# Gathering the rows of the first four expert tiles straight to their places, and moving the remaining gathers, stores and sums of a GNN + top-2 MoE kernel

## The chip, the cores and the metric

The kernel runs on one core of one Trainium2 chip. The metric is the device time of one execution in microseconds (us); lower is better. Engines are named as in the profile: PE (TensorE), DVE (VectorE), ACT (ScalarE), POOL (GpSimd), SP (SyncE, which here only issues DMAs).

## The reference

Two layers on 3125 nodes of 256 features:

```
x = x + segment_sum(einsum('ni,roi->rno', layernorm(x), w)[type, src], dst) + bias     # 53125 edges, 8 relations
n = layernorm(x)
probs = softmax(n @ gate_w + gate_b); top-2 of 16 experts, renormalised
out_e = (silu(n @ w1[e]) * (n @ w2[e])) @ w3[e]                                         # hidden 512
x = x + sum over the two chosen experts of weight * out_e
```

## The kernel before

The first two thirds (up to about 628 us) aggregate the messages of the edges, compute the second layer's normalised rows and gate logits, write these rows to the DRAM table x2_tab and choose the experts. The change does not touch them. It touches the expert stage behind them.

**Tiles.** Each (token, expert) pair has a slot; each expert's slots are padded to whole tiles of 128 rows. Experts are handled in an order of ranks: experts 0 and 1, then the others by number, the two with most tokens last. With the drawn inputs the routing of the reference gives 58 tiles, and the number of tiles up to and including rank 0, 1, 2, ... 15 is

```
rank       0  1  2   3   4   5   6   7   8   9  10  11  12  13  14  15
tiles to   3  6  9  14  16  18  23  26  29  33  37  38  43  45  50  58
```

**A tile j on PE** (expert_tile in the tensor block): turn_hid(j-1) transposes the previous tile's gated rows (line 1536); up(j) multiplies tile j's rows with w1 and w2, 12 matmul pieces (line 1528); turn_xs(j+1) transposes the next tile's rows (line 1494); down(j-1) multiplies the previous tile's gated rows with w3 (line 1510). Before up(j) PE waits for split12 of the tile's expert, before down(j-1) for split3.

**On DVE** for tile j: low_hid(j-1) (line 1253, the low part of the turned gated rows), the product hid(j) (line 1263), low_xs(j+1) (line 1243), copy_y(j-1) from PSUM to the one buffer y_sb (line 1249), which waits until the store of y of tile j-2 has landed. **On ACT** for tile j: high_hid(j-1) (line 744), silu (line 753), high_xs(j+1) (line 739), load_xs(j+2) with its argument counted from that call, that is the load of tile j+3's rows from the DRAM table xs_tab (line 735), and store_y(j-1), which waits for copy_y(j-1) and issues its store to y_tab (line 761).

**Rows.** POOL gathers rows from x2_tab with indirect DMAs, one per tile. Tiles 0 and 1 go straight to the buffers xs (line 572). All tiles, 0 and 1 included, go in "octs" of eight to a buffer (gather_oct: an index copy on line 560, eight gathers on line 564), from which SP stores them in two halves to xs_tab (store_oct, line 476); ACT's load_xs reads them back one at a time. gather_oct(q) waits for the second store of oct q-1.

**Weights.** For each rank e from 2 on, POOL runs in this order: the octs from oct_end[e-1] to oct_end[e]-1, then split_expert(e), which cuts the raw weights into a high and a low part (lines 551 and 553; first the w1 and w2 part, signalling split12, then the w3 part, signalling split3). The first part waits for the raw weights and for the up of the last tile of rank e-2, whose buffer it takes. SP runs in this order: load_expert(e) (three DMAs, line 445) once split e-2 is done, then the stores of the same octs, each of which it waits for. Rank 0 and 1 are split by ACT and DVE at the start (split_first, line 1198).

**Behind the octs** POOL gathers, 25 times each, the y rows of every token's lower and higher slot (lines 602 and 615). DVE adds the first set to acc (add_first, line 1312; 25 in all, 6 or 7 behind each of the last four tiles), ACT copies the sums to PSUM (keep_sum, line 788), DVE adds the second set (line 1331), SP and ACT store the output (lines 501 and 797).

oct_end of a rank is (tiles to + 7) >> 3 for ranks 2 to 14 and (58 + 11) >> 3 for rank 15; for ranks 0 and 1 it is 1. So oct 0 stands ahead of everything and octs 1 to 7 stand ahead of the splits of ranks 2, 5, 7, 9, 12, 14 and 15.

Of the kernel before, what the change touches and what calls it, by code (L numbers as in the profile page):

```python
# [29 lines left out]
I32 = mybir.dt.int32  # L30
ALU = mybir.AluOpType
# [3 lines left out]
P = 128  # L35
NODES, DIM, RELS = 3125, 256, 8
EDGES = 53125
EXPERTS, HIDDEN = 16, 512
# [4 lines left out]
TILES = NODES // TP  # L43
# [31 lines left out]
SLOTS = SLOT_TILES * P  # L75
AHEAD = 3
OCT = 8
HALF_OCT = OCT // 2
OCTS = -(-(SLOT_TILES + AHEAD) // OCT)
XS_TILES = OCTS * OCT  # L80
ZT = 7
# [3 lines left out]
LAST_PAIRS = 2  # L85
# [9 lines left out]
def build(nc, x, src, dst, etype, w_rel, b_rel, gate_w, gate_b, w1, w2, w3, out):  # L95
# [5 lines left out]
    with ExitStack() as ctx:  # L101
        def sb(name, shape, dt=F32):
            return ctx.enter_context(nc.sbuf_tensor(name, shape, dt))

        def sem(name):
            return ctx.enter_context(nc.semaphore(name))
# [130 lines left out]
        slot_hot = got_room[:, got_hots:got_hots + 2 * TILES * SLOT_TILES].rearrange("p (n h) -> p n h", h=SLOT_TILES)  # L237
        token = sb("token", [P, XS_TILES], I32)
        first_idx = sb("first_idx", [P, 2], I32)
        oct_idx = sb("oct_idx", [P, OCT], I32)  # L240
# [114 lines left out]
        slot_free = sem("slot_free")  # L355
        xs_first = [sem(f"xs_first{n}") for n in range(2)]
        xs_in = [sem(f"xs_in{n}") for n in range(2)]
# [148 lines left out]
        def _(pool):  # L506
# [50 lines left out]
            def gather_oct(q):  # L557
                pool.wait_ge(xs_stored, (q * 2 + 1) * 16)
                pool.sem_inc(slot_free, 1)
                nc.gpsimd.tensor_copy(oct_idx[:, :], token[:, bass.ds(q * OCT, OCT)]).then_inc(oct_ready, 1)  # L560
                pool.wait_ge(oct_ready, q + 1)
                pool.sem_inc(slot_free, 1)
                for u in range(OCT):
                    nc.gpsimd.indirect_dma_start(  # L564
                        xg[:, u, :], None, x2_tab,
                        bass.IndirectOffsetOnAxis(ap=oct_idx[:, u:u + 1], axis=0)).then_inc(oct_got[u // HALF_OCT], 16)
# [54 lines left out]
        def _(act):  # L621

            for free in (moved_on, tail_clear, x2_kept):
                act.sem_inc(free, 1)
            act.sem_inc(y_stored, 16)
            act.wait_ge(zero_set, 1)

# [105 lines left out]
            def load_xs(j, s):  # L733
                act.wait_ge(xs_stored, (j // HALF_OCT + 2) * 16)
                act.dma_start(xs[:, s, :], xs_tab[bass.ds(j * P, P), :]).then_inc(xs_in[s], 16)

            def high_xs(j, s):
                act.wait_ge(xs_turned, j + 1)
                nc.scalar.copy(xsT[:, 0, :, :], ps[:, XS_BANK, 0:DIM].rearrange("p (k n) -> p k n", k=KT)).then_inc(xsT_high, 1)
                load_xs(j + 2, s)  # L740
# [5 lines left out]
            def expert_tile(i, u, first=False):  # L746
# [18 lines left out]
            final_j = act.value_load(final[0:1, 0:1], min_val=0, max_val=SLOT_TILES - 1)  # L765
            pairs = act.value_load(pairs_i[0:1, 0:1], min_val=EXPERTS // 2, max_val=SLOT_TILES // 2)
            high_xs(0, 0)
            act.wait_ge(pos_done, 1)
            expert_tile(0, 0, first=True)
            expert_tile(0, 1)  # L770
            with act.Fori(1, pairs) as i:
                for u in range(2):
                    expert_tile(i, u)
            act.wait_ge(y_done, final_j + 1)
            high_hid(final_j)
            store_y(final_j)
            act.wait_ge(xs_in[0], (pairs + 1) * 16)
            act.wait_ge(xs_in[1], pairs * 16)
# [24 lines left out]
        def _(dve):  # L803
            steps = [0]

            def step(ins):

                steps[0] += 1
                ins.then_inc(vec_step, 1)
                dve.wait_ge(vec_step, steps[0])  # L810
# [371 lines left out]
            dve.wait_ge(inv_summed, 1)  # L1182
            v.tensor_scalar(first_idx[:, :], ps[:, INV_BANK, 0:2], float(MID_TOKEN), None, ALU.add).then_inc(token_done, 1)
            v.tensor_scalar(token[:, 0:SLOT_TILES], ps[:, INV_BANK, 0:SLOT_TILES], float(MID_TOKEN), None, ALU.add).then_inc(token_done, 1)
# [129 lines left out]

            early = dve.value_load(early_i[0:1, 0:1], min_val=EXPERTS // 2 - LAST_PAIRS, max_val=SLOT_TILES // 2 - LAST_PAIRS)
            with dve.Fori(3, early) as i:
# [19 lines left out]
        def _(pe):  # L1336
# [150 lines left out]

            def turn_xs(i, u, first=False):
                if first:
                    pe.wait_ge(xs_first[u], 16)  # L1490
                else:
                    pe.wait_ge(xs_in[u], i * 16)
                for k in range(KT):
                    last = nc.tensor.transpose(ps[:, XS_BANK, k * P:(k + 1) * P], xs[:, u, k * P:(k + 1) * P], ident[:, :])
                last.then_inc(xs_turned, 1)
# [42 lines left out]

            def expert_tile(i, u, first=False):
# [11 lines left out]
                turn_xs(i + u, 1 - u, first=first)  # L1551
# [10 lines left out]
            expert_tile(0, 1)  # L1562
            with pe.Fori(1, pairs) as i:
                for u in range(2):
                    expert_tile(i, u)
# [22 lines left out]
```

## Time and profile before

| what | value |
|---|---|
| three runs | 974.35, 977.85, 988.51 us; median 977.85 us |
| profiled execution | 975.37 us, of which the span from the first to the last instruction is 973.7 us |
| share of the span busy | PE 78%, POOL 68%, DVE 52%, ACT 27% |
| mean granted TensorE clock | 0.887 of full speed |

The span is what the profile's times are counted in; 1.7 us of the execution's time lie around it. A timeline row gives start, duration (us), engine, line, operation, output<-input, and in brackets how long the engine had been idle and what ended that.

### The profile page before, as it was taken

The page shows a single profiled execution, that of the slowest core. Times are in us where ns is not written, and L with a number is a line of the kernel's source. Part 1 is how long each engine was busy: PE and PEld are TensorE (multiplying, and loading weights), DVE is VectorE, ACT ScalarE, POOL GpSimd, SP SyncE. Part 2 cuts the span into 40 slices and gives each one's busy share as a digit, 9 for nine tenths or more (in the row PEclk, how much of TensorE's full clock was granted, in tenths as well). Part 3 has the DMA queues.
Part 4 walks back from the last instruction along what each step waited for, and adds up shares of the span by engine and source line. Part 5 has one row for each costly group of instructions (what it writes and reads, how often), then busy time and mean ns, then how long its engine had stood idle before and what let it go on. Part 6 is the DMA issues. An engine that isn't in the chain of part 4 may idle for free.

```text
span 973.7 us, 18213 instructions
## 1 busy us (share of the span) xinstructions
PE 755.4 (78%) x4527; PEld 633.7 (65%) x4528; DVE 504.2 (52%) x1473; ACT 263.0 (27%) x397; POOL 663.7 (68%) x621
## 2 busy tenths in 40 slices
PE   0446787977779888778888878268999999999981
PEld 0434576766658676666667657257888888888861
DVE  6776444545464444546444576866444344444474
ACT  4821222223222222222222222312322232322223
POOL 1077777777777777777777770156768678688775
PEclk9765998989889798988889999569999999999995
DMA  8534444444454333343334332148465665656457
GB/s 206 177 100 144 141 145 141 141 144 140 141 175 130 103 107 102 105 131 103 107 102 132 104 103 99 64 149 277 132 207 169 204 202 181 209 174 221 140 149 221
DMA packets 93343, 144.16 MB, mean 148 GB/s; under 512 B 13335, under 2 KB 67563, under 8 KB 93322
## 3 DMA queue, kind: packets, MB, share of 16 engines
q0 software_dynamic: 25968, 70.94, 25.1%
q1 hardware_dynamic: 49856, 57.31, 18.4%
q10 hardware_dynamic: 17498, 15.68, 5.0%
q8 instruction: 7, 0.11, 0.1%
q14 instruction: 14, 0.11, 0.0%
HBM read 109.90 MB, written 33.98 MB: 148 GB/s over the span
## 4 chain that ended last, share of the span: by engine, by line
PE 48%; DMA 14%; issue 12%; POOL 9%; DVE 8%; DVEq 3%; ACT 3%; ACTq 1%; SPq 0%; POOLq 0%
PE ps L1390 16%; PE ps L1528 12%; PE ps L1378 9%; PE ps L1510 7%; DMA got<-x_tab,idx 7%; POOL got L528 5%; DMA y_tab<-ffn 4%; PE ps L1536 2%; POOL part L553 2%; DMA acc<-in_x 2%; ACT store L683 1%; PE ps L1420 1%; DVE hot L947 1%; POOL x_sb L564 1%; DVE store L965 1%
## 5 line engine op out<-in xcount | busy, mean ns | idle before, releaser
L528 POOL DMA_INDIRECT got<-x_tab,idx x425 | 405.1, 953 | 172.3 <-issue 153.7
L1378 PE MATMUL ps<-hot,got 125*128 125x256 f16 x1700 | 235.1, 301 | 112.4 <-DMA got<-x_tab,idx 90.7
L1378 PEld LDWEIGHTS ps<-hot,got 125*128 125x128 f16 x1700 | 176.3, 106 | 166.9 <-issue 113.3
L965 DVE TENSOR_TENSOR store<-store,ps 128x512 f32 x150 | 102.6, 684 | 237.0 <-PE ps L1378 209.4
L1390 PE MATMUL ps<-part,store 128*128 128x256 f32 x800 | 190.5, 398 | 0.5 <-DVE acc L978 0.5
L1528 PE MATMUL ps<-part,operands 128*128 x696 | 181.2, 410 | 3.2 <-POOL part L553 2.0
L1390 PEld LDWEIGHTS ps<-part,store 128*128 128x128 f32 x800 | 159.4, 202 | 22.9 <-issue 0.5
L1528 PEld LDWEIGHTS ps<-part,operands 128*128 128x128 f32 x696 | 130.2, 193 | 31.3 <-issue 4.0
L947 DVE TENSOR_SCALAR hot<-key_row,pass,drel 125x256 f16<-125x256 f16 x425 | 123.1, 357 | 10.1 <-issue 10.1
L1510 PE MATMUL ps<-part,operands 128*128 x696 | 100.4, 294 | 13.7 <-DVE operands L1253 13.1
L666 ACT ACTIVATE dev<-mv,eps 125x1 f32<-125x1 f32 x25 | 7.4, 295 | 356.1 <-DVE mv L985 356.1
L1510 PEld LDWEIGHTS ps<-part,operands 128*128 128x128 f32 x696 | 89.2, 193 | 16.5 <-issue 16.5
L553 POOL TENSOR_TENSOR part<-store,part 128x2048 fp32r<-128x2048 f32 (+1 forms) x28 | 98.2, 3507 | 2.3
L564 POOL DMA_INDIRECT x_sb<-x_tab,oct_idx x64 | 61.8, 965 | 23.4 <-issue 16.5
L1253 DVE TENSOR_TENSOR operands<-ps,operands 128x512 fp32r<-128x512 f32 x58 | 40.1, 691 | 71.5 <-ACT operands L744 71.4
L744 ACT CAST operands<-ps 128x512 fp32r<-128x512 f32 x58 | 34.1, 587 | 158.2 <-DVE ffn L1249 140.6
L683 ACT COPY store<-store (+1 forms) x24 | 54.2, 2259 | 50.9 <-DVE store L965 50.9
L551 POOL TENSOR_SCALAR part<-store 128x2048 fp32r<-128x2048 f32 (+1 forms) x28 | 42.0, 1500 | 36.5 <-PE ps L1528 16.5
L1263 DVE TENSOR_TENSOR ffn<-ffn,ps 128x512 f32<-128x512 f32 x58 | 39.8, 685 | 38.8 <-PE ps L1528 32.5
L1249 DVE COPY ffn<-ps 128x256 f32<-128x256 f32 x58 | 24.6, 425 | 57.6 <-PE ps L1510 42.3
L661 ACT COPY store<-zero 128x2000 f32 (+1 forms) x25 | 46.8, 1874 | 0.0
L1536 PE MATMUL ps<-ident,ffn 128*128 128x128 f32 x232 | 35.7, 277 | 7.2 <-DVE ffn L1263 7.2
(225 smaller groups left out, 580.7 us busy)
## 6 DMA issues: line engine op xcount, KB each, us to landing
store<-in_L_ffn_w SPq DMA_DIRECT2D x48, 512.0 KB, 5.1
xs_tab<-x_sb SPq DMA_DIRECT2D x16, 512.0 KB, 3.3
y_tab<-ffn SPq DMA_DIRECT2D x9, 896.0 KB
ffn<-xs_tab ACTq DMA_DIRECT2D x59, 128.0 KB
y_tab<-ffn ACTq DMA_DIRECT2D x58, 128.0 KB
got<-x_tab,idx POOLq DMA_INDIRECT x425, 2.8
acc<-in_x SPq DMA_DIRECT2D x5, 560.0 KB
x_tab<-got SPq DMA_DIRECT2D x5, 560.0 KB
```

The lines of the kernel that those rows point to most:

```text
L528: nc.gpsimd.indirect_dma_start(got[:, c, :], None, x_tab, bass.IndirectOffsetOnAxis(ap=idx[:, c:c + 1], axis=0)).then_inc(gathered[c], 16)
L553: nc.gpsimd.tensor_tensor(part[:, 2 * k + 1, at:at + cols], whole, high.bitcast(F32), ALU.subtract).then_inc(done, 1)
L564: nc.gpsimd.indirect_dma_start(xg[:, u, :], None, x2_tab, bass.IndirectOffsetOnAxis(ap=oct_idx[:, u:u + 1], axis=0)).then_inc(oct_got[u // ...
L661: nc.scalar.copy(buffer(i, SPAN - TP, SPAN), zero[:, 0:1].unsqueeze(1).to_broadcast([P, KT * RELS, TP])).then_inc(tail_clear, 1)
L683: nc.scalar.copy(buffer(i + 1, 0, SPAN - TP), buffer(i, TP, SPAN)).then_inc(moved_on, 1)
L947: v.tensor_scalar(hot[0:CE, g % HOT, c - GROUPS[g][0], :], key_row[0:CE, :], pass0[0:CE, 0:1], drel[0:CE, bass.ds(turn * TC + c, 1)], ALU. ...
L965: v.tensor_tensor(window, window, ps[:, WIN_BANK[g], :].rearrange("p (q n) -> p q n", n=WIN), ALU.add).then_inc(win_added, 1)
L1378: last = mm(ps[:, WIN_BANK[g], k * KEYS:(k + 1) * KEYS], got[0:CE, c, a * DIM + k * P:a * DIM + (k + 1) * P], hot[0:CE, g % HOT, c - c0, : ...
L1390: last = mm(ps[:, bank, 0:DIM], sums[:, at, k, r, 0:P], wT[:, k, r * DIM:(r + 1) * DIM], start=(r == 0 and k == 0), stop=(r == RELS - 1 an ...
L1510: last = mm(ps[:, Y_BANK, 0:DIM], hidT[:, a, k, :], part3[:, bass.ds(at + b, 1), k, :].rearrange("p a n -> p (a n)"), start=(k == 0 and a ...
L1528: last = mm(ps[:, UP_BANK + w, :], xsT[:, a, k, :], part12[:, bass.ds(at + b, 1), w, k, :].rearrange("p a n -> p (a n)"), start=(k == 0 an ...
L1536: last = nc.tensor.transpose(ps[:, HID_BANK, k * P:(k + 1) * P], hid[:, k * P:(k + 1) * P], ident[:, :])
```

## The change

Five edits in the expert stage. (1) Four tiles instead of two are gathered straight to buffers (two new ones, xs_ahead), and oct q holds tiles 4+8q to 11+8q. PE takes tiles 0 to 3 from the buffers; ACT's first load is that of tile 4, issued in tile 1, and in tile 0 ACT loads nothing. (2) oct_end becomes max(tiles to + 4, 8) >> 3 for ranks 0 to 14 and (58 + 4) >> 3 = 7 for rank 15: seven octs, 1 to 6 standing ahead of the splits of ranks 3, 6, 8, 10, 13 and 15. (3) ACT's store_y(j-2) stands behind high_hid(j-1) in tile j, no longer at the end of tile j-1. (4) The loads past the last tile are left out. (5) DVE's 25 add_first stand behind the last low_hid: three ahead of the last copy_y, 22 behind it.

```diff
-AHEAD = 3
+DIRECT = 4
-OCTS = -(-(SLOT_TILES + AHEAD) // OCT)
+OCTS = -(-(SLOT_TILES + 2 - DIRECT) // OCT)
...
-                nc.gpsimd.tensor_copy(oct_idx[:, :], token[:, bass.ds(q * OCT, OCT)]).then_inc(oct_ready, 1)
+                nc.gpsimd.tensor_copy(oct_idx[:, :], token[:, bass.ds(q * OCT + DIRECT, OCT)]).then_inc(oct_ready, 1)
...
-            for u in range(2):
+            for u in range(DIRECT):
                 nc.gpsimd.indirect_dma_start(
-                    xs[:, u, :], None, x2_tab,
+                    xs[:, u, :] if u < 2 else xs_ahead[:, u - 2, :], None, x2_tab,
                     bass.IndirectOffsetOnAxis(ap=first_idx[:, u:u + 1], axis=0)).then_inc(xs_first[u], 16)
...
             def load_xs(j, s):
-                act.wait_ge(xs_stored, (j // HALF_OCT + 2) * 16)
+                act.wait_ge(xs_stored, (j // HALF_OCT + 1) * 16)
...
-                high_xs(j + 1, 1 - u)
-                if not first:
-                    store_y(j - 1)
+                if not first and not second:
+                    store_y(j - 2)
                 act.wait_ge(up1_done, j + 1)
                 act.wait_ge(hid_ready, j)
                 nc.scalar.activation(gate, ps[:, UP_BANK, :], ACT.Silu).then_inc(gate_ready, 1)
                 act.wait_ge(up2_done, j + 1)
+                high_xs(j + 1, 1 - u, load=load and not first)
...
             act.wait_ge(y_done, final_j + 1)
             high_hid(final_j)
+            store_y(final_j - 1)
             store_y(final_j)
...
-                v.tensor_scalar(oct_f[:, EXPERTS - 1:], t_rank[:, EXPERTS - 1:EXPERTS], float(OCT + AHEAD), None, ALU.add)
-                step(v.tensor_scalar(oct_f[:, 0:EXPERTS - 1], t_rank[:, 0:EXPERTS - 1], float(OCT - 1), None, ALU.add))
+                v.tensor_scalar(oct_f[:, EXPERTS - 1:], half_f[:, :], 2.0, float(OCT - DIRECT), ALU.mult, ALU.add)
+                step(v.tensor_scalar(oct_f[:, 0:EXPERTS - 1], t_rank[:, 0:EXPERTS - 1], float(OCT - DIRECT), float(OCT), ALU.add, ALU.max))
...
-            last_tiles = 2 * LAST_PAIRS
-            for n in range(last_tiles):
-                expert_tile(early + n // 2, n % 2)
-                for t in range(TILES * n // last_tiles, TILES * (n + 1) // last_tiles):
-                    add_first(t)
             low_hid(final_j)
+            for t in range(3):
+                add_first(t)
             copy_y(final_j)
+            for t in range(3, TILES):
+                add_first(t)
...
-            turn_xs(0, 0, first=True)
-            expert_tile(0, 0, first=True)
-            expert_tile(0, 1)
-            with pe.Fori(1, pairs) as i:
+            turn_xs(0, 0, direct=True)
+            expert_tile(0, 0, first=True, direct=True)
+            expert_tile(0, 1, direct=True)
+            expert_tile(1, 0, direct=True)
+            expert_tile(1, 1)
+            with pe.Fori(2, pairs) as i:
```

## Rows read from the trace of the kernel before

**Rows 1.** The page's first part: busy us, share of the span, count of instructions.
```profile
PE 755.4 (78%) x4527; PEld 633.7 (65%) x4528; DVE 504.2 (52%) x1473; ACT 263.0 (27%) x397; POOL 663.7 (68%) x621
```

**Rows 2.** Timeline, PE: up of tiles 1, 9, 13, 18 and 57.
```profile
646.91 5.26 PE L1528 MATMUL ps<-part,operands 128*128 x12
...
693.75 3.05 PE L1528 MATMUL ps<-part,operands 128*128 x12
...
713.41 3.05 PE L1528 MATMUL ps<-part,operands 128*128 x12
...
740.11 3.07 PE L1528 MATMUL ps<-part,operands 128*128 x12
...
939.90 3.05 PE L1528 MATMUL ps<-part,operands 128*128 x12
```

**Rows 3.** Timeline, POOL: index copies of octs 2 and 3, and their splits.
```profile
702.34 0.19 POOL L560 COPY oct_idx<-token 128x8 int32 x1
...
716.74 1.92 POOL L551 TENSOR_SCALAR part<-store 128x2048 fp32r<-128x2048 f32 x1 [3.62 <-issue]
718.75 4.62 POOL L553 TENSOR_TENSOR part<-store,part 128x2048 fp32r<-128x2048 f32 x1
...
730.34 1.91 POOL L551 TENSOR_SCALAR part<-store 128x2048 fp32r<-128x2048 f32 x1 [3.46 <-DMA store<-in_L_ffn_w]
...
740.36 0.18 POOL L560 COPY oct_idx<-token 128x8 int32 x1
...
751.15 1.92 POOL L551 TENSOR_SCALAR part<-store 128x2048 fp32r<-128x2048 f32 x1
...
758.87 2.39 POOL L553 TENSOR_TENSOR part<-store,part 128x1024 fp32r<-128x1024 f32 x1
```

**Rows 4.** Timeline, start of the stage: POOL's copy, SP's load, split of rank 2.
```profile
649.37 0.43 POOL L560 COPY oct_idx<-token 128x8 int32 x1 [5.15 <-DMA xs_tab<-x_sb]
...
651.83 2.36 SPq L445 DMA_DIRECT2D store<-in_L_ffn_w  x3
...
662.32 1.94 POOL L551 TENSOR_SCALAR part<-store 128x2048 fp32r<-128x2048 f32 x1 [2.00 <-DMA store<-in_L_ffn_w]
```

**Rows 5.** Timeline of SP alone: loads of ranks 6 and 7.
```profile
723.07 6.07 SPq L445 DMA_DIRECT2D store<-in_L_ffn_w  x6
```

**Rows 6.** Timeline, start of the stage: two gathers of POOL beside DVE's subtractions.
```profile
629.72 2.27 DVE L1198 TENSOR_TENSOR part<-store,part 128x2048 fp32r<-128x2048 f32 x1
...
630.34 2.48 POOL L572 DMA_INDIRECT ffn<-x_tab,first_idx  x1 [0.30 <-issue]
...
638.02 1.30 DVE L1198 TENSOR_TENSOR part<-store,part 128x1024 fp32r<-128x1024 f32 x1
638.06 0.94 POOL L564 DMA_INDIRECT x_sb<-x_tab,oct_idx  x1 [0.30 <-issue]
```

**Rows 7.** Timeline, start of the stage: DVE's tables and ACT's first silu.
```profile
640.92 0.06 DVE L1238 MEMSET oct_end<- 1x2 int32 x1
...
644.77 0.60 ACT L753 ACTIVATE ffn<-ps 128x512 f32<-128x512 f32 x1 [11.88 <-DMA xs_tab<-x_sb]
```

**Rows 8.** Waits, 640 to 954 us: us in total, times, longest.
```profile
DVE ffn L1249 <- DMA y_tab<-ffn: 15.3, 8, 3.0
```

**Rows 9.** Timeline, end: POOL's first and last y gather, last tile, final adds.
```profile
903.96 1.00 POOL L602 DMA_INDIRECT x_sb<-y_tab,pos  x1 [0.15 <-issue]
...
945.73 2.85 DVE L1312 SCALAR_TENSOR_TENSOR acc<-x_sb,wts,acc 125x256 f32<-125x256 f32 x7
...
949.50 2.93 PE L1510 MATMUL ps<-part,operands 128*128 x12 [3.81 <-DVE operands L1253]
...
954.19 7.37 DVE L1331 SCALAR_TENSOR_TENSOR acc<-store,wts,ps 125x256 f32<-125x256 f32 x17 [1.20 <-ACT ps L788]
...
966.10 0.95 POOL L615 DMA_INDIRECT store<-y_tab,pos  x1 [0.30 <-issue]
...
970.83 0.48 DVE L1331 SCALAR_TENSOR_TENSOR acc<-store,wts,ps 125x256 f32<-125x256 f32 x1 [1.15 <-DMA store<-y_tab,pos]
```

More of the change, by code:

```diff
@@ L237, in build @@
         slot_hot = got_room[:, got_hots:got_hots + 2 * TILES * SLOT_TILES].rearrange("p (n h) -> p n h", h=SLOT_TILES)
-        token = sb("token", [P, XS_TILES], I32)
-        first_idx = sb("first_idx", [P, 2], I32)
+        token = sb("token", [P, XS_TILES + DIRECT], I32)
+        first_idx = sb("first_idx", [P, DIRECT], I32)
+        xs_ahead = sb("xs_ahead", [P, DIRECT - 2, DIM])
         oct_idx = sb("oct_idx", [P, OCT], I32)
@@ L355, in build @@
         slot_free = sem("slot_free")
-        xs_first = [sem(f"xs_first{n}") for n in range(2)]
+        xs_first = [sem(f"xs_first{n}") for n in range(DIRECT)]
         xs_in = [sem(f"xs_in{n}") for n in range(2)]
@@ L625, in _ @@
             act.sem_inc(y_stored, 16)
+            for n in range(2):
+                act.sem_inc(xs_in[n], (n + 1) * 16)
             act.wait_ge(zero_set, 1)
@@ L733, in load_xs, with high_xs @@
             def load_xs(j, s):
-                act.wait_ge(xs_stored, (j // HALF_OCT + 2) * 16)
-                act.dma_start(xs[:, s, :], xs_tab[bass.ds(j * P, P), :]).then_inc(xs_in[s], 16)
-            def high_xs(j, s):
+                act.wait_ge(xs_stored, (j // HALF_OCT + 1) * 16)
+                at = nc.s_assert_within(j - DIRECT, 0, XS_TILES - 1, skip_runtime_bounds_check_because="pairs are counted from 1")
+                act.dma_start(xs[:, s, :], xs_tab[bass.ds(at * P, P), :]).then_inc(xs_in[s], 16)
+            def high_xs(j, s, load=True):
                 act.wait_ge(xs_turned, j + 1)
                 nc.scalar.copy(xsT[:, 0, :, :], ps[:, XS_BANK, 0:DIM].rearrange("p (k n) -> p k n", k=KT)).then_inc(xsT_high, 1)
-                load_xs(j + 2, s)
+                if load:
+                    load_xs(j + 2, s)
             def high_hid(j):
@@ L744, in high_hid, with expert_tile @@
                 nc.scalar.copy(hidT[:, 0, :, :], ps[:, HID_BANK, :].rearrange("p (k n) -> p k n", k=HT)).then_inc(hidT_high, 1)
-            def expert_tile(i, u, first=False):
+            def expert_tile(i, u, first=False, second=False, load=True):
                 j = i * 2 + u
@@ L764, in _ @@
             act.sem_inc(tiles_begun, 1)
-            final_j = act.value_load(final[0:1, 0:1], min_val=0, max_val=SLOT_TILES - 1)
+            final_j = act.value_load(final[0:1, 0:1], min_val=EXPERTS - 1, max_val=SLOT_TILES - 1)
             pairs = act.value_load(pairs_i[0:1, 0:1], min_val=EXPERTS // 2, max_val=SLOT_TILES // 2)
-            high_xs(0, 0)
+            early = act.value_load(early_i[0:1, 0:1], min_val=EXPERTS // 2 - LAST_PAIRS, max_val=SLOT_TILES // 2 - LAST_PAIRS)
+            high_xs(0, 0, load=False)
             act.wait_ge(pos_done, 1)
             expert_tile(0, 0, first=True)
-            expert_tile(0, 1)
-            with act.Fori(1, pairs) as i:
+            expert_tile(0, 1, second=True)
+            with act.Fori(1, early + (LAST_PAIRS - 1)) as i:
                 for u in range(2):
                     expert_tile(i, u)
+            for u in range(2):
+                expert_tile(early + (LAST_PAIRS - 1), u, load=False)
             act.wait_ge(y_done, final_j + 1)
             high_hid(final_j)
+            store_y(final_j - 1)
             store_y(final_j)
-            act.wait_ge(xs_in[0], (pairs + 1) * 16)
+            act.wait_ge(xs_in[0], pairs * 16)
             act.wait_ge(xs_in[1], pairs * 16)
@@ L1182, in _ @@
             dve.wait_ge(inv_summed, 1)
-            v.tensor_scalar(first_idx[:, :], ps[:, INV_BANK, 0:2], float(MID_TOKEN), None, ALU.add).then_inc(token_done, 1)
+            v.tensor_scalar(first_idx[:, :], ps[:, INV_BANK, 0:DIRECT], float(MID_TOKEN), None, ALU.add).then_inc(token_done, 1)
             v.tensor_scalar(token[:, 0:SLOT_TILES], ps[:, INV_BANK, 0:SLOT_TILES], float(MID_TOKEN), None, ALU.add).then_inc(token_done, 1)
@@ L1313, in add_first @@
                                        in1=acc[:, t, :], op0=ALU.mult, op1=ALU.add).then_inc(part_done, 1)
-            early = dve.value_load(early_i[0:1, 0:1], min_val=EXPERTS // 2 - LAST_PAIRS, max_val=SLOT_TILES // 2 - LAST_PAIRS)
-            with dve.Fori(3, early) as i:
+            with dve.Fori(3, pairs) as i:
                 for u in range(2):
                     expert_tile(i, u)
-            last_tiles = 2 * LAST_PAIRS
-            for n in range(last_tiles):
-                expert_tile(early + n // 2, n % 2)
-                for t in range(TILES * n // last_tiles, TILES * (n + 1) // last_tiles):
-                    add_first(t)
             low_hid(final_j)
+            for t in range(3):
+                add_first(t)
             copy_y(final_j)
+            for t in range(3, TILES):
+                add_first(t)
             for t in range(TILES):
@@ L1485, in _, with turn_xs @@
             pe.wait_ge(owner_done, 3)
-            def turn_xs(i, u, first=False):
-                if first:
-                    pe.wait_ge(xs_first[u], 16)
-                else:
-                    pe.wait_ge(xs_in[u], i * 16)
+            def turn_xs(i, u, direct=False):
+                if direct:
+                    pe.wait_ge(xs_first[2 * i + u], 16)
+                else:
+                    pe.wait_ge(xs_in[u], (i + u) * 16)
+                rows = xs_ahead if direct and i else xs
                 for k in range(KT):
-                    last = nc.tensor.transpose(ps[:, XS_BANK, k * P:(k + 1) * P], xs[:, u, k * P:(k + 1) * P], ident[:, :])
+                    last = nc.tensor.transpose(ps[:, XS_BANK, k * P:(k + 1) * P], rows[:, u, k * P:(k + 1) * P], ident[:, :])
                 last.then_inc(xs_turned, 1)
@@ L1537, in turn_hid, with expert_tile @@
                 last.then_inc(hid_turned, 1)
-            def expert_tile(i, u, first=False):
+            def expert_tile(i, u, first=False, direct=False):
                 j = i * 2 + u
@@ L1550, in expert_tile @@
                 owner_at(coming, j + 1)
-                turn_xs(i + u, 1 - u, first=first)
+                turn_xs(i + u, 1 - u, direct=direct)
                 if not first:
@@ L1559, in _ @@
             owner_at(this, 0)
-            turn_xs(0, 0, first=True)
-            expert_tile(0, 0, first=True)
-            expert_tile(0, 1)
-            with pe.Fori(1, pairs) as i:
+            turn_xs(0, 0, direct=True)
[4 more added lines that the diff above has]
+            with pe.Fori(2, pairs) as i:
                 for u in range(2):
```

## The prediction

> **What bounds the kernel now.** I read the page first: PE is busy for 78% of the span and POOL for 68% [rows 1], so in the expert stage either may set the end. The timeline of PE then gives the pace. Between tile 18 (740.11) and tile 57 (939.90) 199.8 us pass for 39 tiles [rows 2]; where nothing stalls, tile 9 to tile 13 takes 19.66 us, 4.9 us a tile, so 191.2 of the 199.8 us are PE's own pace and 8.6 us are stalls. Stretches between waits are PE-bound; the stalls come from two sides. One is the store of y: DVE's copy waited 8 times, 15.3 us in all, for a store that had not landed [rows 8]. The other is POOL.
>
> POOL's timeline shows its prices. An oct takes 10.8 us from its index copy (740.36) to the next split (751.15). A split takes 10.1 us (751.15 to 758.87 + 2.39), and its first part, which releases PE's up, 6.6 us (716.74 to 718.75 + 4.62) [rows 3]. From an oct's index copy (702.34) through its two stores and SP's next load (723.07) to the split that needs this load (730.34) it is 28.0 us [rows 3, 5]; it is one of four such passages (octs 2 to 5), between 26.1 and 28.0 us, and I use 27. At the end POOL issues 50 gathers without a gap from 903.96 to 966.10, and the last adds and output stores follow [rows 9]. So PE stops at 952.4 but the kernel ends at 973.7: **the end is set by when POOL is through its last split**, 0.2 us before 903.96, as long as PE is not much later.
>
> **The start (edits 1 and 3).** ACT's first silu waited 11.88 us for oct 0's first store, because the load of tile 2 stood ahead of it in ACT's queue. That load is gone. DVE's product of tile 0 then waits only for DVE itself, which is busy with tables to 640.98, instead of for the silu that ends at 645.37 [rows 7]: 4.4 us earlier. From tile 1 (646.91) to tile 9 (693.75) 46.8 us pass for 8 tiles [rows 2]; 39.2 are pace, so 7.6 were lost there, 2.2 of them to the clock (below) and the rest to y stores that met rank 2's load and to DVE's weight sums. With the store behind high_hid and the first y stores ahead of that load, I take 3.6 of these back: 8 us of lead in all, between 4.4 and 10. Alone this would be the gain.
>
> **The octs (edits 1 and 2).** The two extra gathers stand ahead of oct 0: 2 x 1.27 us (49 steps from 903.96 to 966.10 [rows 9]). The eight gathers of oct 0 now lie beside DVE's two subtractions of split_first(1). One gather beside such an operation took 2.48 us and another 0.94 us [rows 6], so this costs 0 to 1.5 us for each of two; I take 1.5 in all. Oct 0 is stored 4 us later, and SP, which waits for it, issues rank 2's load at 655.8 instead of 651.83 [rows 4].
>
> The Trainium skill's page "SBUF — State Buffer", section "SBUF: two separate sides", says GpSimd cannot write a gather's descriptors while a VectorE operation holds the shared port pair. The 2.48 us gather that ends 0.8 us after the subtraction agrees, the 0.94 us one beside the subtraction of 638.02 does not. By the rule both subtractions would block, and the load would be issued 1.5 us later than I take.
>
> Now the order matters. Before, oct 1 was gathered while rank 2's load was still under way and cost nothing: copy at 649.37, split 2 at 662.32 [rows 4]. After the change rank 2 has 9 + 4 = 13, 13 >> 3 = 1, so oct 1 stands behind split 2 and ahead of split 3, and POOL stands idle for the load. The load took 10.5 us to its split beside oct 1's gathers and 7.3 us elsewhere (723.07 to 730.34) [rows 3 to 5]; I take 7.5 us, split 2 at 663.3. Then 10.2 (split 2) + 10.8 (oct 1) + 6.6 (first part of split 3) + 0.2 puts **up of tile 9 at 691.1**. PE would want it at 685.7 (8 us ahead of 693.75): a new wait of 5.4 us that takes most of the lead, 2.6 us left against 693.75 [rows 2]. After such an idle time PE ran at 1.2 GHz: the up of tile 1, behind a long wait, took 5.26 us against 3.05 us at 2.4 GHz, and the last down took 2.93 us after 3.81 us idle [rows 2, 9]. That is 2.2 us more. Tile 13 is at 691.1 + 2.2 + 19.6 = 712.9, where it was before (713.41).
>
> Split 5 needs the up of tile 13 (tiles to rank 3 are 14), so it starts 3.3 us later, 716.2, as before. Before, oct 2 lay ahead of it in idle time. Now it lies behind it, ahead of split 6: 716.2 + 10.2 + 10.8 + 6.6 + 0.3 puts **up of tile 18 at 744.1, 4.0 us later than before**, after 6.7 us of idle PE, and again 2.2 us at 1.2 GHz: 6.2 us behind.
>
> From there the cycle runs oct, store, load, split (27.0), the even split (10.2), next oct: oct 2 at 726.4, oct 3 at 763.6, oct 4 at 800.8, split 11 at 827.8, split 12 at 838.0, oct 5 at 848.2, split 14 at 875.2 with its first part done at 881.8. Splits 7 to 13 are ready when PE comes, within 1 us. Tile 45 needs split 14: 882.1, against PE's own 744.1 + 2.2 + 27 x 4.9 = 878.6. Then tile 57 at 940.9 (before 939.90). Split 14 ends at 885.4, oct 6 and split 15 take 10.8 + 10.2: **POOL is free at 906.4, 2.6 us later** than before, although it has one oct (10.8 us) less to do: it has exchanged that for idle time behind loads.
>
> **The store behind high_hid (edit 3).** After a late copy ACT issued the store and then high_hid, and DVE's low part waited for that; now DVE goes on at once, but each store is issued later by high_hid's time, and so lands later. Its worth lies between a small loss and the 8.6 us of stalls. I count the y stalls behind tile 18 as gone, since I added none to the sum; this is not seen at the end, because the splits bind there.
>
> **The end (edit 5).** The last four tiles lose their adds: at least most of the 3.81 us that PE stood idle ahead of the last down, behind seven adds [rows 9]. Before, the last down began 9.6 us after tile 57's up; without that wait, and at 2.4 GHz, it ends near 950 instead of 952.4. One copy later, 22 adds of 0.41 us (2.85 us for seven) take 9.0 us, to 959.6, and 25 final adds of 0.43 us (7.37 us for 17) take 10.8, to 970.4. The last gather is issued at 966.10 + 2.6 = 968.7, and its add starts 4.7 us later as before (970.83), at 973.4. So POOL is still last, by 3 us, and the output stores, which started at 954 and now start at 960, are packed closer: 0.8 us, taken between 0 and 2.
>
> **Sum.** 2.6 + 0.8 = 3.4 us on the profiled execution's 975.37: 978.8 us. The three runs' median, 977.85, is 2.5 above the profiled execution, but with one run at 988.51 in it; I put half of that on: 980.
>
> **The rivals.** (A) *The lead is kept, faster.* Rank 2's load is issued 1.5 us earlier and PE's clock does not fall at tiles 9 and 18: 1.5 + 4.4 us off the chain, POOL free some 3 to 5 us before 903.96. If the new waits are shorter too, the freed oct shows, POOL would be done near 895, PE's last copy near 945, and the 22 adds in front of 25 final ones become the bound: 945 + 9.0 + 10.8, 2.9 for the last output store (970.83 to 973.7) and 1.7 around the span, that is 969.4; 971 with the packed stores. For it: POOL loses an oct and 8 us at the start are real. Against it: both octs 1 and 2 leave idle time for busy time [rows 3, 4].
>
> (B) *The loads are slow, slower.* Everything behind hangs on rank 2's load and on four store-load passages. If the first takes the 10.5 us it took before [rows 4] and each passage the 28.0 us of the row instead of 27, that is 3 + 4 us, and with the port rule 1.5 more: 988. It decides once POOL is free after 908. To pass 2% (997) POOL would have to be free after 922; no row carries that.
>
> (C) *Nothing reaches the end.* POOL is free within 1 us of 903.8 since losses and the oct cancel, or the moved adds are the only thing seen: 976 to 978.
>
> **Chances.** Forecast 0.45, A 0.2, B 0.15, C 0.2. The range 969 to 990 holds the forecast, C, most of A and B. A change of 2% is about what a measurement of this kernel can tell from none; 958 and 997 are beyond all cases but their mixtures: faster 0.04, same 0.92, slower 0.04.
>
> **What would show it.** First silu near 638 and tile 1's up near 642.5: the start. A PE wait of 4 to 7 us ahead of tile 9 ended by POOL's subtraction of split 3, another ahead of tile 18, with an up of 5 us behind each: the octs' places. First y gather at 905 to 908: the end. It is wrong if POOL is free before 900, if tile 18 comes before 740, or if the final adds are released by ACT and not by gathers.

## The result and the profile after

The changed kernel takes 983.07 us (median of 20 runs, 980.78 to 987.2) against 979.24 us (median of 20 runs, 973.25 to 988.51) for the kernel before. The ratio is 1.0041, interval 1.0023 to 1.0059: **0.4%, or 4.0 us, slower** (3.8 us between the medians), beyond the noise and far inside 2%. The profiled execution took 984.52 us with a span of 982.8 us. Each ratio, here and below, uses only the executions that took at most 1.5% longer than the fastest of their kernel; of the kernel before in the set of 1228.2 us, below, these are 5 of 23.

PE's timeline of the changed kernel, the ups of tiles 1, 6, 13, 18, 45 and 57 (the up matmuls are on line 1535 here):

```profile
642.53 4.17 PE L1535 MATMUL ps<-part,operands 128*128 x12
...
677.84 3.64 PE L1535 MATMUL ps<-part,operands 128*128 x12
...
712.58 3.05 PE L1535 MATMUL ps<-part,operands 128*128 x12
...
743.74 4.70 PE L1535 MATMUL ps<-part,operands 128*128 x12 [6.46 <-POOL part L554]
...
882.09 2.14 PE L1535 MATMUL ps<-part,operands 128*128 x8 [2.86 <-POOL part L554]
...
940.63 3.05 PE L1535 MATMUL ps<-part,operands 128*128 x12
```

Tile 1 comes 4.4 us earlier than before (646.91), tile 13 only 0.8 us earlier (713.41), and tile 18 comes 3.6 us later (740.11) [rows 2], behind 6.46 us in which PE stood idle for POOL's split. At tile 57 it is 0.7 us later.

POOL's timeline of the changed kernel, the split of rank 2, the index copies of octs 1 and 2, the split of rank 6 and the first y gather:

```profile
663.44 1.91 POOL L552 TENSOR_SCALAR part<-store 128x2048 fp32r<-128x2048 f32 x1 [15.87 <-DMA store<-in_L_ffn_w]
...
673.40 0.18 POOL L561 COPY oct_idx<-token 128x8 int32 x1
...
726.21 0.19 POOL L561 COPY oct_idx<-token 128x8 int32 x1 [0.18 <-issue]
...
736.95 1.92 POOL L552 TENSOR_SCALAR part<-store 128x2048 fp32r<-128x2048 f32 x1
...
906.27 1.00 POOL L603 DMA_INDIRECT x_sb<-y_tab,pos  x1
```

The first row shows the price of the new order: POOL stood idle for 15.87 us, for a load, at a place where it gathered oct 1 before [rows 4]. Although it has an oct less to gather, POOL is through its last split 2.3 us later than before (first y gather at 906.27 instead of 903.96 [rows 9]).

The end of the same timeline, with DVE and the output stores:

```profile
949.91 8.79 DVE L1320 SCALAR_TENSOR_TENSOR acc<-x_sb,wts,acc 125x256 f32<-125x256 f32 x22
...
954.67 4.84 POOL L616 DMA_INDIRECT store<-y_tab,pos  x1 [0.30 <-issue]
...
972.33 0.95 POOL L616 DMA_INDIRECT store<-y_tab,pos  x1 [0.30 <-issue]
...
977.42 0.48 DVE L1337 SCALAR_TENSOR_TENSOR acc<-store,wts,ps 125x256 f32<-125x256 f32 x1 [1.84 <-DMA store<-y_tab,pos]
```

One y gather took 4.84 us instead of 0.95. It ended at 959.51, 0.8 us after DVE's block of 22 sums (958.70). The 11 gathers behind it follow 1.25 us apart, so that in this kernel the last gather depends on the end of that block too, and the block stands behind PE's last tile. From the first to the last y gather it is 66.1 us, before 62.1 [rows 9]: 3.9 us more. 2.3 + 3.9 us put the last gather 6.2 us later, and its add 6.6 us later (977.42, before 970.83). The spans differ by 9.1 us: in single executions the time behind the last add varies too (2.4 us before, 4.9 us here), and this execution lies 1.5 us above its kernel's median while that of before lies 3.9 us below. So the traces show where time can go, and the 4.0 us of the ratio say how much it came to; how they divide among the causes is not shown.

### The profile page after: what moved, and what is told of

The parts are those of the page before. It is cut to its first block, busy times and chain, and to the rows that moved or that the text cites. A ratio compares the mean times of both kernels' runs of the same rounds, so it can differ in the third digit from the quotient of the medians.

```text
span 982.8 us, 18144 instructions
## 1 busy us (share of the span) xinstructions
PE 753.0 (77%) x4527; PEld 631.4 (64%) x4528; DVE 511.8 (52%) x1473; ACT 266.5 (27%) x397; POOL 660.9 (67%) x614
## 4 chain that ended last, share of the span: by engine, by line
PE 48%; issue 13%; DMA 11%; POOL 11%; DVE 9%; DVEq 3%; ACT 3%; SPq 1%; POOLq 1%; ACTq 0%
PE ps L1396 15%; PE ps L1535 14%; PE ps L1384 7%; PE ps L1517 7%; POOL got L529 7%; DMA got<-x_tab,idx 6%; ACT store L686 2%; PE ps L1543 2%; DMA acc<-in_x 2%; POOL part L554 1%; DVE store L973 1%; DVE hot L955 1%; POOL x_sb L565 1%; PE ps L1501 1%; PE ps L1426 1%
## 5 line engine op out<-in xcount | busy, mean ns | idle before, releaser
L565 POOL DMA_INDIRECT x_sb<-x_tab,oct_idx x56 | 54.6, 975 | 20.5 <-issue 14.6
L760 ACT ACTIVATE ffn<-ps 128x512 f32<-128x512 f32 x58 | 34.7, 598 | 63.8 <-PE ps L1535 52.8
```

The source lines that it names most:

```text
L565: nc.gpsimd.indirect_dma_start(xg[:, u, :], None, x2_tab, bass.IndirectOffsetOnAxis(ap=oct_idx[:, u:u + 1], axis=0)).then_inc(oct_got[u // ...
```

## Experiments

The kernels were timed in four sets, each with the kernel before beside them: first e1 to e4; then a0, e1 and e3 again, and e5; then e7 and e8; last e9 and e1 a third time. The kernel before took 1185.8 and 1228.2 us in the first two sets (21 and 23 runs) and 976.3 and 977.7 us in the last two. In the slow sets the expert stage itself began late (up of tile 0 at 783.12 us in the changed kernel's trace of the second set, at 633.76 in its first trace), and POOL waited 27.5 us for y stores in its second set of gathers, instead of 0.3 us. The second and the third set are on record with the same chip number, so this is not shown to be a property of a chip, as some of the expectations take it; why it happens is open. Ratios are to the kernel before in the same set. The changed kernel itself was timed anew only in the second set.

The stretch ahead of the expert stage also varies from one execution to the next: the up of tile 0 is at 633.68 us in the kernel before, 633.76 in the changed kernel, 632.58 in e7, 633.38 in e8, 632.30 in e9 and 630.68 in the third e1. Where kernels are compared by their traces, times counted from tile 0 are therefore given beside those of the rows.

### The first sums back, and the first sums alone

Theory P says that the block of sums on DVE keeps GpSimd (POOL) from issuing its gathers. Theory O says that all of the loss lies in the places of the octs.

```diff
 # e1: the changed kernel with
-            low_hid(final_j)
-            for t in range(3):
-                add_first(t)
-            copy_y(final_j)
-            for t in range(3, TILES):
-                add_first(t)
+            for n in range(last_tiles):
+                expert_tile(early + n // 2, n % 2)
+                for t in range(TILES * n // last_tiles, TILES * (n + 1) // last_tiles):
+                    add_first(t)
+            low_hid(final_j)
+            copy_y(final_j)
 # e2: the kernel before with the opposite edit
```

> The changed kernel with the 25 first sums back behind the last four tiles. Theory P (the block of 22 adds on DVE keeps GpSimd from issuing its y gathers: one took 4.84 us and ended 0.8 us after the adds): no y gather over 1.3 us, the 50 gathers take 62.1 us again instead of 66, the last one is issued near 968.5 us instead of 972.3, and the time is 3 to 5 us under the changed kernel's, about equal to the kernel before. Theory O (all of the loss lies in the places of the octs, POOL free 2.2 us later): the time is as the changed kernel's within 1.5 us, since the last gathers would be held by the last tiles, which the adds delay by 1.4 us again.

> The kernel before with this one edit: three first sums ahead of the last copy of y, 22 behind it. Theory P: PE's last down ends 3 us earlier (near 949), one y gather is stretched to 3 to 5 us beside the 22 adds, the last gather is issued near 970 instead of 966.1, and the time is 3 to 5 us above the kernel before. Theory O: nothing at the end but the moved adds, POOL stays in step, time equal to the kernel before within 1 us.

Measured in the set of 1185.8 us: e1 0.9853 (0.981 to 0.9897), e2 1.0033 (1.0000 to 1.0067), which is 3.9 us where P put 3 to 5, with an interval that reaches down to O's nothing. The views by line of the second set's gathers (durations in ns, least, median and most), first e1, then e2:

```profile
L616 POOL DMA_INDIRECT store<-y_tab,pos x25: 940/946/1072, 1101.7 to 1151.6; - x25
```

```profile
L615 POOL DMA_INDIRECT store<-y_tab,pos x25: 942/946/6677, 1127.2 to 1180.3; - x25
```

One edit on the otherwise unchanged kernel makes one gather of 6.68 us; taking it out of the changed kernel removes it. Over all traces, five of seven with the block of 22 sums have one gather of 4.84 to 6.68 us (the first trace of the changed kernel, a0, e2, e5 and e7), and none of seven with the sums apart has one over 1.3 us. In all five the gather ends 0.81 to 0.82 us after the last sum of the block. So the block brings the stretched gather about. It is not enough for it alone: e3 and its repeat, below, keep the block and have no gather over 1.28 us. What it costs does not show well here, because these gathers also wait 24 to 25 us for y stores. Why e1 is 1.5% faster than the kernel before in this set, and not in the later ones, is open; the store of y, below, is a candidate. The same kernel was run twice more, with the changed kernel beside it and then in a set with the times of the first result:

> The changed kernel itself, beside the others on one chip, since the first four were timed on a chip where the kernel before takes 1185.8 us instead of 979. If the chip is like the first one: 1.002 to 1.006 of the kernel before. If it is like the second, where DMAs land later: theory P and O both leave it between the kernel before and the kernel with the adds back, 0.985 to 1.0, since late y stores are what the later store position forgives.

> The changed kernel with the first sums back behind the last four tiles, again. Theory P: no y gather over 1.3 us, last gather issued 3.5 to 4 us earlier than in the changed kernel on the same chip, time 3 to 5 us less. Theory O: within 1.5 us of the changed kernel.

> The changed kernel with the first sums back behind the last four tiles, once more, for a chip on which DMAs land early. Theory P: POOL free as in the changed kernel (906 us), no gather of 4.8 us, last gather issued near 968.5 us instead of 972.3, time 3 to 5 us under the changed kernel's 983, that is 0.998 to 1.003 of the kernel before. Theory O: 1.004 or more.

In the set of 1228.2 us a0 is 0.9969 (0.9887 to 1.0051) and e1 0.9956 (0.9876 to 1.0037), which tells nothing apart. The earlier last gather that P promised did not come there: e1's is issued at 1175.17 and a0's at 1170.46, both behind waits for y stores. In the set of 977.7 us e1 is 1.0012 (0.9985 to 1.0039), against the changed kernel's 1.0041 (1.0023 to 1.0059) in the first result: 0.29%, 2.8 us less, at the low edge of what P said, with intervals that overlap; O's 1.004 or more lies just outside e1's. Its first and last y gather:

```profile
903.01 1.00 POOL L603 DMA_INDIRECT x_sb<-y_tab,pos  x1 [0.15 <-issue]
...
965.12 0.95 POOL L616 DMA_INDIRECT store<-y_tab,pos  x1 [0.30 <-issue]
```

These are 62.1 us again, and no gather takes over 1.3 us. Counted from tile 0, the first y gather comes 272.3 us later, in the changed kernel 272.5, and the last one 334.4 us later instead of 338.6: 4.1 us less. So in these two traces the block is worth those 4.1 us at the last gather. That all of it reaches the time is not shown. That some does is supported by e7, below, which keeps the block: its 1.0074 (1.0050 to 1.0099) and e1's interval do not meet. The two also differ by six small operations, whose move made e7's trace shorter neither at tile 18 nor at the first y gather.

### The places of the octs

```diff
 # e3: the changed kernel with
-                step(v.tensor_scalar(oct_f[:, 0:EXPERTS - 1], t_rank[:, 0:EXPERTS - 1], float(OCT - DIRECT), float(OCT), ALU.add, ALU.max))
+                step(v.tensor_scalar(oct_f[:, 0:EXPERTS - 1], t_rank[:, 0:EXPERTS - 1], float(OCT - 1), float(OCT), ALU.add, ALU.max))
 # e4: e3 and e1 together
```

> The changed kernel with the octs ahead of the splits of ranks 2, 5, 7, 9, 12 and 14 as before (seven octs, four direct tiles, all else as changed). Theory O: tile 6 is no longer held by DVE and the late load, tile 18 comes at 732 to 736 us instead of 743.7, split 15 follows split 14 without an oct between them but waits for rank 15's load, POOL is free near 899 to 901 instead of 906.2, and the time is 4 to 7 us under the changed kernel's. Theory P alone (the places matter little since POOL and the loads are in a cycle anyway): POOL free within 1.5 us of 906, time within 1.5 us of the changed kernel's.

> Both: the octs in their places of before and the first sums behind the last four tiles. If P and O both hold the gains add up: POOL free near 900, 50 gathers in 62.1 us, last gather near 962.5, time 8 to 11 us under the changed kernel's and 4 to 7 us under the kernel before. If only one holds, the time is as that one's kernel alone. If PE is then the bound (last down near 946 to 950), the last gathers wait for the last store and the gain stops at about 6 us.

> The changed kernel with the octs' places of before, again. Theory O: tile 18 near 732 to 736 us, POOL free near 899 to 901, time 4 to 7 us less than the changed kernel on the same chip. Theory P alone: POOL free within 1.5 us of the changed kernel's, time within 1.5 us.

In the set of 1185.8 us: e3 0.9814 (0.9777 to 0.9852), e4 0.9801 (0.9749 to 0.9853). In the set of 1228.2 us: e3 0.9899 (0.9808 to 0.999), where the changed kernel is 0.9969 (0.9887 to 1.0051). The two pairs that differ by the places alone, e4 against e1 (0.9853) and the repeat of e3 against the changed kernel, show the old places faster by 0.5 and 0.7%, with overlapping intervals, and e4, which has both edits, is not clear of e3. e3 and its repeat keep the block of 22 sums. POOL's timeline of e3 beside that block (1136.22 to 1145.01):

```profile
1139.29 0.99 POOL L616 DMA_INDIRECT store<-y_tab,pos  x1 [0.52 <-issue]
1140.59 1.27 POOL L616 DMA_INDIRECT store<-y_tab,pos  x1 [0.30 <-issue]
1146.30 0.94 POOL L616 DMA_INDIRECT store<-y_tab,pos  x1 [4.43 <-DVE acc L1337]
```

Here a gather begun 4.4 us into the block (1140.59) takes 1.27 us, where one begun 4.8 us into it in the changed kernel takes 4.84. But the next one has to wait 4.43 us: its place comes free with a final add (L1337), and that add stands behind the block in DVE's queue. So the block holds POOL here too, by an order of work and not inside an instruction. Why one gather is stretched and the other not stays open. The times in us that were expected rest on the first result's traces and can't be held against these. The places are taken up again with e8, below.

### The store of y

```diff
 # e5: the changed kernel with
-                if not first and not second:
-                    store_y(j - 2)
                 act.wait_ge(up1_done, j + 1)
...
                 high_xs(j + 1, 1 - u, load=load and not first)
+                if not first:
+                    store_y(j - 1)
...
             high_hid(final_j)
-            store_y(final_j - 1)
```

> The changed kernel with ACT's store of y back at the end of the tile, ahead of the next high_hid. If the later store forgives late landings but the splits bind (my prediction): PE stalls of 1 to 2 us come back at the tiles whose store lands over 4.3 us, POOL's splits stay where they are, the time is within 1.5 us of the changed kernel's. Rival: the later store is itself the cost at tiles 4 to 6, where DVE waited for a store and its low part came at 673.41 us: then tile 6 comes earlier without it and the time falls by 1 to 3 us.

Measured in the set of 1228.2 us: 1.0124 (0.9972 to 1.0276), against 0.9969 of the changed kernel. The two were expected within 1.5 us of each other; the later place of the store looks worth 1.5% in this set, but the intervals overlap, so this is a hint. The rival, that the later store is the cost at tiles 4 to 6, falls: tile 6 came 13.4 us after tile 5 with the store back too (14.2 in a0). What holds tile 6 is in the next section.

### The six small operations

The changed kernel has a stall that I had not foreseen, at tile 6. Its timeline, POOL, DVE and PE:

```profile
665.43 4.56 POOL L554 TENSOR_TENSOR part<-store,part 128x2048 fp32r<-128x2048 f32 x1
...
665.63 5.40 DVE L1313 TENSOR_SCALAR upto<-upto_i,t_rank 1x25 f32<-1x25 int32 x2
...
671.09 2.36 POOL L554 TENSOR_TENSOR part<-store,part 128x1024 fp32r<-128x1024 f32 x1
...
671.28 2.21 DVE L1315 CAST pos<-low_hi 125x50 int32<-125x50 f32 x1
...
673.41 0.68 DVE L1261 TENSOR_TENSOR operands<-ps,operands 128x512 fp32r<-128x512 f32 x1
...
674.41 2.92 PE L1517 MATMUL ps<-part,operands 128*128 x12 [7.32 <-DVE operands L1261]
```

Two operations on one partition and 25 numbers, 0.23 us each in the kernel before, take 5.40 us together (4.39 and 0.98): each ends within 0.1 us of the end of the POOL operation beside it (669.99, then 671.01). They stand in DVE's queue ahead of the low part of tile 4, so PE waits 7.32 us. The kernel before ran them from 674.4 us on, when the split was over; the changed kernel is 10.4 us ahead by then and runs into it. The Trainium skill's page "SBUF — State Buffer", section "SBUF: two separate sides", says that DVE and GpSimd share a port pair under an exclusive lock, and that whichever starts first has it for the whole instruction while the other is blocked. These rows agree, with one reserve: on DVE's side the section names operations in a two-port mode or with two inputs in SBUF, and no run shows in which mode the small ones ran. The gather of 4.84 us goes beyond that sentence: it was held across some ten sums of 0.4 us each and not for one, while others beside the same block took 0.95 to 1.27 us.

A row of this kind stood in the kernel before, beside its split 2 (POOL from 662.32 [rows 4]):

```profile
662.54 1.76 DVE L1292 TENSOR_TENSOR wts<-wts,mtx 125x25 f32<-125x25 f32 x1
```

The same operation took 0.19 us at 662.00, ahead of the split. The low part of tile 2 stood behind it in DVE's queue there, so the hold that later cost 7 us could be read from the kernel before.

```diff
 # e7: the changed kernel with
             expert_tile(2, 0)
-            <upto_i, upto, need, pos2: six operations>
             expert_tile(2, 1)
+            expert_tile(3, 0)
+            <the same six operations>
+            expert_tile(3, 1)
```

> The changed kernel with DVE's six small operations for the y gathers (upto, need, pos2) behind the first half of pair 3 instead of pair 2, so that they come when rank 2's split on POOL is over. Theory L (these operations are held by POOL's split through a lock between the two engines, 10 us at tile 6): each of them takes 0.2 us again, tile 6 starts as soon as the first part of split 2 is done, 7 us earlier. What it brings: if my prediction's chain is right, tile 9 then waits about 6 us for split 3, which stands behind oct 1, so that tile 13, tile 18 and the end stay within 1 us and the time within 1.5 us of the changed kernel's. Rival: the 7 us are kept and the time falls by 5 us or more, since the places of the octs cost nothing.

Measured: 1.0074 (1.0050 to 1.0099), where the kernel before takes 976.3 us. The small operations are no longer held (the cast takes 0.19 us), tile 6 comes at 669.43 instead of 677.84 (36.8 us after tile 0 instead of 44.1), and nothing is won. PE's and POOL's timeline of e7 at tile 9:

```profile
685.38 4.49 POOL L554 TENSOR_TENSOR part<-store,part 128x2048 fp32r<-128x2048 f32 x1
...
690.16 5.48 PE L1537 MATMUL ps<-part,operands 128*128 x12 [5.85 <-POOL part L554]
```

This is the wait that the prediction put there: 5.85 us for split 3, behind oct 1, and an up of 5.48 us behind it (tile 9 at 690.16; 691.1 was forecast). The granted clock of PE was 0.51 of full speed from 690.1 to 695.7 us. Tile 18 is at 743.40, in the changed kernel at 743.74; counted from tile 0 these are 110.8 and 110.0 us. The stall at tile 6 had only stood in place of this wait. Why e7 is 0.3% above the changed kernel, where at most 1.5 us were expected, is open; the intervals (1.0023 to 1.0059 and 1.0050 to 1.0099) overlap.

### All three, and the sums spread

e8 puts the octs and the sums back and keeps the six operations behind the first tile of pair 3 (tile 6). e9 is e8 with `LAST_PAIRS = 4` instead of 2, that is 3 or 4 sums behind each of the last eight tiles.

> The changed kernel with three things put back or moved: the octs in their places of before, the first sums behind the last four tiles, the six small operations behind the first half of pair 3. If places, adds and lock are three separate costs, this is the fastest of all: no operation of DVE and no y gather over 1.5 us, tile 13 at least 6 us earlier relative to tile 0 than in the changed kernel, POOL free 5 to 8 us earlier, time 8 to 12 us under the changed kernel's where DMAs land as early as on the first chip, and 2 to 3% under the kernel before where they land late. Rival: the lead is used up by y stores and loads, and it equals the kernel with places and adds put back within 0.3%.

> The kernel with the octs' old places, the six small operations moved and the first sums put back, with one more edit: the 25 sums are spread over the last eight tiles (3 or 4 behind each) instead of four (6 or 7). In that kernel the last down came at 950.72 us because of seven adds, and the final adds were released by ACT and not by gathers. If the end there is PE and DVE: the last down comes at 946 to 948 us, no tile is stretched by adds (4.9 us each instead of 5.5), the time falls by 2 to 4 us, to 0.990 to 0.996 of the kernel before, until the last gather (issued at 960.2, landing near 965) sets the end. Rival: the output stores are the bound, and the time falls by less than 1 us.

e8: 0.9970 (0.9936 to 1.0005), median 972.16 us against 976.31; against e7 in the same set 0.9970 / 1.0074 = 0.990, 1.0% or 10 to 12 us less, with intervals that don't meet. So octs and sums together cost e7 that much. Its POOL timeline from oct 6's index copy to the first y gather:

```profile
861.87 0.19 POOL L561 COPY oct_idx<-token 128x8 int32 x1 [0.17 <-issue]
...
872.64 1.92 POOL L552 TENSOR_SCALAR part<-store 128x2048 fp32r<-128x2048 f32 x1
...
887.83 1.91 POOL L552 TENSOR_SCALAR part<-store 128x2048 fp32r<-128x2048 f32 x1 [5.16 <-DMA store<-in_L_ffn_w]
...
898.09 1.01 POOL L603 DMA_INDIRECT x_sb<-y_tab,pos  x1
```

With the old places the freed oct shows: no oct stands between the last two splits, and POOL is through at 897.9, against 904.9 in e7. Tile 18 is at 737.18, 6.2 us earlier than in e7 (7.0 counted from tile 0); at tile 13, counted so, e8 is 2.4 us ahead of e7 and only 1.6 us ahead of the changed kernel, where at least 6 were expected. e7 and e8 both have the direct tiles and the small operations moved, and the sums come later than this point, so the 7 us at POOL's last split go with the places in these two traces. They are not a fixed price: e9, the same kernel up to its last tiles, was through at 902.9 (below). e8's last gather is issued at 960.19, yet the end comes only at 971.0:

```profile
950.72 1.85 PE L1521 MATMUL ps<-part,operands 128*128 x12 [3.81 <-DVE operands L1261]
...
964.82 1.47 DVE L1341 SCALAR_TENSOR_TENSOR acc<-store,wts,ps 125x256 f32<-125x256 f32 x3 [0.33 <-ACT ps L796]
```

Now the last down, held by seven sums to 950.72 us, and the final adds, released by ACT, are the chain. The gain stops there.

e9 was to take that away and came out at 0.9983 (0.9954 to 1.0011), no better than e8 and above the 0.990 to 0.996 that were expected. The tiles near the end are 4.88 us apart as expected, but the last down came at 951.51 and not at 946 to 948. Split 2 began 11.0 us after the issue of rank 2's load, in e8 8.7 us after it, so it slid by 1.6 us, and the six operations met a POOL split again, now that of rank 3. DVE's and PE's timeline of e9:

```profile
682.17 5.56 DVE L1315 TENSOR_SCALAR upto<-upto_i,t_rank 1x25 f32<-1x25 int32 x2
...
687.97 2.21 DVE L1317 CAST pos<-low_hi 125x50 int32<-125x50 f32 x1
...
691.10 2.92 PE L1521 MATMUL ps<-part,operands 128*128 x12 [7.89 <-DVE operands L1261]
```

PE stands 7.89 us for DVE, and the up behind that comes 14.6 us after the one before it (694.53 behind 679.93). So whether the small operations are free depends on a DMA's landing, and the sums' spreading stays untested at the end that it was meant for. POOL was through its last split at 902.9 us, that is 270.6 us after tile 0, where e7 has 272.3 and e8 264.6: of the 7.7 us between e7 and e8 1.7 are left in this trace. Beside e9 in its set the third e1 took 0.3% more (1.0012), with overlapping intervals. Neither e8 nor e9 is clear of the kernel before.

## Why the prediction was right, point by point

The time, 983.07 us, is inside the stated 969 to 990 us, but that range runs from 0.9% faster to 1.2% slower, so meeting it says little; the points below weigh more. Against the rivals: the lead was not kept (A), POOL was not late enough for slow loads (B, 906.1 where it needed 908), and POOL's last split moved by more than 1 us (C).

**What bounds the kernel.** Right up to POOL's last split: the end follows it, and the shift there was 2.3 us, 2.6 forecast. Behind it DVE's block of sums came in, which the prediction had left out (below, at the end).

**The start.** Right: first silu at 638.14, tile 1 at 642.53 (642.5 forecast), 4.4 us earlier; tile 4 at 658.36, 10.4 us earlier than before, just past the far end of my 4.4 to 10.

**The gathers of oct 0.** Rank 2's load was issued at 655.75 (655.8 forecast) and its split began at 663.44 (663.3). Of the gathers beside DVE's subtractions one took 2.08 us, ending 0.8 us after the subtraction, and the others 0.94 to 1.07: between two held gathers, as I had applied the port rule, and none.

**Oct 1 behind split 2.** The time was right, the place not. Tile 13 came at 712.58 (712.9 forecast), but PE's wait was at tile 6, for DVE's small operations held by split 2, and not at tile 9 for split 3. The step that failed is the one that sent PE undisturbed from tile 4 to tile 9, to want the latter at 685.7: I had looked only at what the split signals, not at what runs beside it, and had put the 1.76 us of the kernel before down to "DVE's weight sums". With the small operations moved (e7) the forecast wait appeared. That the two stalls bring tile 13 to nearly the same time (78.8 us after tile 0 here, 79.6 in e7) is luck.

**Oct 2 behind split 5.** Right: tile 18 at 743.74 (744.1 forecast) after 6.46 us idle (6.7), with an up of 4.70 us and tile 19 6.5 us later, 1.7 us above the pace where 2.2 were put.

**The cycle of loads and splits.** Right: tile 45 at 882.09 (882.1), tile 57 at 940.63 (940.9), POOL through at 906.1 (906.4).

**The store behind high_hid.** Right for the trace: between tiles 21 and 44 all but two tiles are 4.9 us apart, although DVE's copy waited for stores more often than before. That the stalls behind tile 18 are gone because of the store's place is not tested at these speeds (e5 ran only in the slow set). The waits of the changed kernel:

```profile
DVE ffn L1257 <- DMA y_tab<-ffn: 18.9, 11, 3.0
```

These are 11 waits and 18.9 us against 8 and 15.3 [rows 8], and nearly none of them stretches a tile.

**The end.** Here a term was mis-sized. I put the packed output stores at 0.8 us, and had nothing for the sums' effect on POOL, though the row of a gather held beside a DVE operation was in my hand [rows 6]: 22 sums in a row held POOL for 3.9 us, in the one stretch where POOL's gathers set the end. That makes 2.3 + 3.9 us at the last gather against 2.6 forecast, and the time behind the last add grew by 2.5 us where 0.8 were put; the spans of the two traces differ by 9.1 us. That the sum of 3.4 us meets the measured 4.0 is in part luck: the medians show less than the two single traces do. The forecast of 980 us is 3.1 us under the measured 983.07.

## What to carry to other kernels

In this kernel work that an engine did while it waited for a transfer cost nothing; moved behind that transfer, the same work cost its full time, and having less of it did not make up for that (one oct less, POOL later). When an edit makes one engine earlier, ask what it now runs beside: small VectorE operations and GpSimd's long ones, or a block of VectorE sums and GpSimd's gathers, can hold each other. A stall that vanishes without a gain (e7) points to the next wait in the same chain, so compute that chain to its end before moving anything. And count the times of two traces from the same event, here tile 0, before calling a difference a gain.

## What the runs showed that I had not expected

- A VectorE operation on one partition and 25 elements took 4.39 us instead of 0.23, beside a GpSimd subtraction of 4.56 us; a cast of 125x50 took 2.21 instead of 0.19.
- A gather issued beside 22 VectorE sums back to back took 4.84 us (4.84 in e7, 5.2 to 6.7 us in three others), while the gathers just ahead of it, beside the same block, took 0.95 to 1.27; in e3, which has the same block, none was over 1.3 us in either of its two traces, nor in any kernel with the sums apart. Why is open. Each stretched gather ended 0.8 us after the block, as the 2.48 us gather of [rows 6] ended 0.8 us after its subtraction.
- The same kernel took 977 us in some sets and 1186 or 1228 us in others, with longer waits for y stores; edits of 0.5% could not be told apart there.
